# A two-layer recurrent mixture-of-experts kernel: final combination, load order and output scatters moved by a block, and a reshaped last pass

## The reference, cut to what matters

```
gate_scores = softmax(xn @ Wg + bg);  topk = top 2 of 8 experts, weights normalised
for e in range(8):
    h = gelu(xn @ W1[e] + b1[e])          # 256 -> 1024
    y = h @ W2[e] + b2[e]                 # 1024 -> 256
    output = output + y * combine_w[..., e:e+1]
g = silu(output)
x = x + s * g                             # s: the layer's attention part; x is the result
```

## Time and profile before

| | us |
|---|---|
| median of 3 runs | 1163.1 |
| lowest and highest of them | 1156.14, 1164.56 |
| the profiled execution, its own time | 1147.92 |
| its span | 1145.8 |
| PE busy in the span | 1033.5 (90%) |

### The profile page before, as it was taken

How to read it: one execution, slowest core, us unless ns; L and a number is a source line. 1 busy time by engine, 2 the same in 40 slices (tenths; PEclk the granted TensorE clock), 3 DMA queues, 4 the chain that set the end, 5 groups by cost and what they waited for, 6 DMA issues and landing times.

```text
span 1145.8 us, 16791 instructions
## 1 busy us (share of the span) xinstructions
PE 1033.5 (90%) x6152; PEld 887.7 (77%) x6152; DVE 692.3 (60%) x1494; ACT 528.7 (46%) x1095; POOL 404.3 (35%) x385
## 2 busy tenths in 40 slices
PE   4559899999999984879899999999999999999993
PEld 3347788888888863568788898988888888888882
DVE  7578777777777858587754644474766100137862
ACT  4425654555545536643344545445453233345641
POOL 1036544554455450001233422322231345432344
PEclk9779999999999997997899999999999999999997
DMA  9914335555565428426487755555244679889961
GB/s 302 265 61 148 93 102 175 162 162 176 162 201 184 122 90 270 160 92 232 111 286 280 249 192 187 191 189 189 106 132 182 218 266 342 322 319 337 395 266 65
DMA packets 120401, 228.65 MB, mean 200 GB/s; under 512 B 14938, under 2 KB 103914, under 8 KB 115328
## 3 DMA queue, kind: packets, MB, share of 16 engines
q1 hardware_dynamic: 106448, 189.31, 48.2%
q0 software_dynamic: 13872, 38.27, 10.3%
HBM read 166.98 MB, written 62.79 MB: 201 GB/s over the span
## 4 chain that ended last, share of the span: by engine, by line
PE 74%; DVE 14%; ACT 5%; DMA 3%; issue 2%; POOL 1%; SPq 1%; POOLq 0%; ACTq 0%; DVEq 0%
PE PS L1306 21%; PE PS L1316 20%; PE PS L1205 6%; PE PS L1090 4%; PE PS L1040 3%; PE PS L1144 3%; PE PS L1099 2%; PE PS L1171 2%; PE PS L1215 2%; PE PS L1182 2%; PE PS L1157 2%; DVE stats L1347 2%; PE PS L1281 1%; PE PS L1292 1%; DVE KB L1482 1%
## 5 line engine op out<-in xcount | busy, mean ns | idle before, releaser
L1306 PE MATMUL PS<-xgT,WE 128*128 128x256 f32 (+1 forms) x1248 | 257.5, 364 | 4.3 <-ACT hT L2255 3.6
L2255 ACT ACTIVATE hT<-PS,WE 128x256 f32<-128x256 f32 (+1 forms) x312 | 140.2, 454 | 237.9 <-PE PS L1306 234.8
L1306 PEld LDWEIGHTS PS<-xgT,WE 128*128 128x128 f32 x1248 | 221.4, 192 | 33.5 <-ACT hT L2255 5.7
L1316 PE MATMUL PS<-WE,hT 128*128 128x256 f32 x1104 | 244.6, 379 | 0.0
L1316 PEld LDWEIGHTS PS<-WE,hT 128*128 128x128 f32 x1104 | 207.6, 190 | 26.8
L1909 DVE TENSOR_TENSOR y<-PS,WE 128x512 f32<-128x512 f32 (+1 forms) x38 | 24.3, 640 | 221.2 <-PE PS L1316 221.2
L2355 POOL DMA_INDIRECT xg<-xn_dram,token_of x71 | 74.2, 1045 | 142.2 <-DVE result_of L1825 116.2
L2367 POOL DMA_INDIRECT result<-y,result_of x53 | 53.7, 1013 | 178.6 <-DVE y L1909 171.5
L1040 PE MATMUL PS<-XT,Wf 128*128 128x256 f32 x384 | 93.6, 399 | 3.3 <-ACT Z L2033 3.3
L1040 PEld LDWEIGHTS PS<-XT,Wf 128*128 128x128 f32 x384 | 74.9, 201 | 15.1 <-ACT Z L2033 4.9
L2314 POOL TENSOR_TENSOR prob<-prob,row_sum 128x512 f32<-128x512 f32 x56 | 58.6, 1046 | 60.2 <-DVE row_sum L1520 59.9
(11 more groups left out here) (276 smaller groups left out, 1720.5 us busy)
## 6 DMA issues: line engine op xcount, KB each, us to landing
WE<-in_experts SPq DMA_DIRECT2D x39, 2180.0 KB, 9.4
wgu<-in_w_gate SPq DMA_DIRECT2D x32, 256.0 KB, 2.9
wgu<-in_w_up SPq DMA_DIRECT2D x32, 256.0 KB, 3.2
wdn<-in_w_down SPq DMA_DIRECT2D x32, 256.0 KB, 3.4
result<-zeros SPq DMA_DIRECT2D x16, 512.0 KB, 4.8
xs<-late_dram SPq DMA_DIRECT2D x16, 512.0 KB, 12.9
both<-result SPq DMA_DIRECT2D x16, 512.0 KB, 9.7
table<-zeros POOLq DMA_DIRECT2D x1, 5160.0 KB, 34.1
```

The lines of the kernel that those rows point to most:

```text
L1306: m = e.matmul(PS[:, FIRST_H_BANK + nth % HR, 0:rows], W1[n % WR][:, k, c * P:(c + 1) * P], xgT[:, n % 2, k, 0:rows], start=k == 0, stop=k ...
L1316: m = e.matmul(PS[:, u.bank, j * D:(j + 1) * D], hT[:, n % 2, c, j * P:(j + 1) * P], W2[n % WR][:, c, :], start=c == 0, stop=c == KF - 1)
L2255: e.activation(hT[:, n % 2, c, 0:rows], PS[:, FIRST_H_BANK + (KF * n + c) % HR, 0:rows], ACT.Gelu_apprx_tanh, bias=b1[n % WR][:, c:c + 1], ...
```

## The change

What it does, by part:

1. `load_both(0..2)` is placed ahead of `load_weights(32)` in block 29's list.
2. `MIXED_AT` loses its empty first entry: the quarters are worked in blocks 30 to 35 (one, two, one, two, one, one), each one late block earlier, though not with the same grouping.
3. `load_xs(5..7)` leave the `store` step; they now follow `load_weights` of the block after the one in which the place's quarter was stored: quarter 5's in block 31, quarters 6's and 7's in block 32.
4. The scatters of late blocks 30 to 33 go to block 35's list, those of 34 and 35 to block 36's, that of 36 to block 37's, that of 37 to block 38's, each behind that block's gather `late_other`; that of 38 stays last. As `LAGGED` is 35 now, `late_sum`, `late_gate` and `late_rest` of blocks 34 to 36 change place too: 35's whole pass stands in block 36, ahead of its own `w2` bank's emptying.
5. Last block: the bias is no longer added when the bank is emptied. `late_bias` adds own weight times `b2` to the scaled other row before the matmuls end; `late_end` then has one sum out of PSUM, a half product that needs no gate, and two more instructions behind the gate.

```
-MIXED_AT = [[], [0, 1], [2], [3], [4, 5], [6], [7]]
+MIXED_AT = [[0], [1, 2], [3], [4, 5], [6], [7]]
 LAGGED = EARLY + len(MIXED_AT) - 1
-PUT_FIRST, PUT_SECOND = 4, 6
+PUTS_AT = {LAGGED: range(0, 4), LAGGED + 1: range(4, 6), LAGGED + 2: range(6, 7), LAST: range(7, 8)}
...
-        if n == LAST - 1:
-            for m in range(PUT_FIRST, PUT_SECOND):
-                add("late_put", EARLY + m)
         if EARLY <= n + 1 < NSLOT:
             add("late_other", n + 1)
-        if n == LAST - 2:
-            for m in range(PUT_FIRST):
-                add("late_put", EARLY + m)
-        if n == LAST - 1:
-            for m in range(EARLY + PUT_SECOND, LAST):
-                add("late_put", m)
+        for m in PUTS_AT.get(n, ()):
+            add("late_put", EARLY + m)
+        if n + 1 == EARLY:
+            for q in range(BR):
+                add("load_both", q)
         if n + WR < NSLOT:
...
                 add("load_weights", n + WR)
+        for q in MIXED_AT[n - 1 - EARLY] if EARLY < n <= LAGGED else ():
+            if q + XSR < QUARTERS:
+                add("load_xs", q + XSR)
         if XS_AT <= n < XS_AT + XSR:
             add("load_xs", n - XS_AT)
-        if n + 1 == EARLY:
-            for q in range(BR):
-                add("load_both", q)
...
+        def late_bias():
+            i = LAST - EARLY
+            w.wait_ge(weights_in[LAST % WR], weights1_landed(LAST))
+            w.wait_ge(late_step, late_n.n)
+            for j in range(2):
+                tile = 2 * i + j
+                e.scalar_tensor_tensor(out=other[i % OR][:, j, :], in0=b2[LAST % WR], scalar=own_weight[:, tile:tile + 1],
+                                       in1=other[i % OR][:, j, :], op0=ALU.mult, op1=ALU.add).then_inc(
+                    late_step, late_n.step())
+            wait_place_free(w, LAST)
+
+        def late_end(j):
+            i, u = LAST - EARLY, use["w2_last", j]
+            tile = 2 * i + j
+            z, half, gate = other[i % OR][:, j, :], y1[:, LAST % YR, j, :], gate_late[:, j, :]
+            filled_by(u)
+            w.wait_ge(late_step, late_n.n)
+            e.scalar_tensor_tensor(out=z, in0=PS[:, u.bank, 0:D], scalar=own_weight[:, tile:tile + 1], in1=z, op0=ALU.mult,
+                                   op1=ALU.add).then_inc(late_summed, 1)
+            w.wait_ge(late_summed, tile + 1)
+            e.scalar_tensor_tensor(out=half, in0=z, scalar=0.5, in1=fin[:, tile, D:2 * D], op0=ALU.mult, op1=ALU.mult).then_inc(
+                late_step, late_n.step())
+            w.wait_ge(late_step, late_n.n)
+            w.wait_ge(late_gated, tile + 1)
+            e.scalar_tensor_tensor(out=half, in0=gate, scalar=1.0, in1=half, op0=ALU.add, op1=ALU.mult).then_inc(
+                late_step, late_n.step())
+            w.wait_ge(late_step, late_n.n)
+            e.tensor_tensor(fin[:, tile, 0:D], fin[:, tile, 0:D], half, ALU.add).then_inc(late_ready, 1)
...
                 j, = at
-                u = use["w2_last", j]
                 if j == 0:
                     late_scale(LAST)
-                filled_by(u)
-                w.wait_ge(weights_in[LAST % WR], weights1_landed(LAST))
-                wait_place_free(w, LAST)
-                e.tensor_tensor(y1[:, LAST % YR, j, :], PS[:, u.bank, 0:D], b2[LAST % WR], ALU.add).then_inc(free[u.bank], 1)
-                w.wait_ge(free[u.bank], u.emptied)
-                late_sum(LAST, j)
-                late_rest(LAST, slice(j, j + 1))
+                    late_bias()
+                late_end(j)
...
                 if q + BR < QUARTERS:
                     load_both(q + BR)
-                if q and q - 1 + XSR < QUARTERS:
-                    load_xs(q - 1 + XSR)
```

More of the change, by code:

```diff
@@ L1614, in late_sum @@
             tile = 2 * i + j
-            u = use["w2_last", j] if n == LAST else use["w2", n]
+            u = use["w2", n]
             w.wait_ge(free[u.bank], u.emptied)
```

## The result

The changed kernel takes 1150.16 us (median of 12 runs, 1145.28 to 1155.94), the kernel before 1158.86 us on the same chip (12 runs, 1156.14 to 1164.56): ratio 0.9919, 95% interval 0.9900 to 0.9939. It is 8.7 us faster. Forecast were 1157 us, a range from 1151 to 1165, and a gain of 5.8 us.

The account below looks back on a forecast made before the run. PE was taken to bound the kernel up to a serial tail of 8.91 us; 6.0 - 0.4 + 0.2 = 5.8 us gained, ratio 0.995, scaled from the median 1163.1 to 1157 us, range 1151 to 1165.

Parts of the forecast that it names:

- Scatters spread (part 4): Tail: block 38's gather is issued by 1119.5 us, so VectorE's 5.44 us of idleness before block 38 go entirely.
- Last pass (part 5): Last block: last scatter at 1129.9 against 1135.98 us, a gain of 6.1, taken as 6.0; removed instructions 0.9.
- Sums ahead of weights (part 1): Block 29: second scatter lands in 2.7 us, so the loads of sums leave at 1004.5 instead of 1009.60 us.
- Quarter 0 in block 30 (part 2): Blocks 30 and 31: `both(0)` lands at 1010.5 us, limit 1012.1, no wait; with slow scatters PE waits 3.5 us.
- DMA load (part 3): Block 36's weights: half a megabyte more ahead of them, 0.4 us more wait, bounds 0 to 2.5.
- Block 35's pass in block 36: ScalarE's gate ahead of block 37's GELUs: ready at 1097.7 us, limit 1101; no wait unless the gather is 3 us later.
- The sum: Whole kernel: 6.0 - 0.4 + 0.2 = 5.8 us gained, profiled execution from 1147.92 to 1142.1 us, ratio 0.995.
- No case gains more than 6.5 us, because PE's end stays.: All cases: 6.5 us is the largest gain, since PE's end fixes the rest of the tail.
- the scaling: Whole time: profiled execution is 1.3% below the median 1163.1 us, so 1163.1 x 0.995 = 1157.

Follow-up runs that it names:

- chip 7: Kernel before and changed kernel run again, both unchanged: ratio 0.9944, 1140.3 against 1147.5 us; block 30's `w1` start to last scatter 130.75 against 136.91 us.
- the first trace: Profile of the unaltered changed kernel from the first measurement: execution 1153.15 us, block 30's `w1` start to last scatter 135.02 us against 137.15 before.
- The slow variant: Changed kernel with the three loads of sums behind block 32's weights, as before: ratio 0.9993 to the kernel before.
- With more load: Both kernels with five extra 512 KB writes, one ahead of each of weights 33 to 37: ratios 1.0013 (kernel before) and 0.9999 (changed).
- chip 8: Slower chip, both kernels run unchanged: changed kernel at ratios 0.9922, 0.9932 and 0.9915, the last 1147.8 against 1157.8 us.

## Why the prediction was right and wrong

- **Scatters spread (part 4): right.** Gather of block 38 at +118.2 on chip 7 (forecast: near +118), no idle time of VectorE between blocks 37 and 38. Undone alone: 2.68 us of the gain.
- **Last pass (part 5): right.** 2.75 us from PE's end to the last scatter (forecast 2.8), 6.16 us gained where 6.0 were taken.
- **Sums ahead of weights (part 1): right**, and shown by undoing it: the scatters land in 2.4 us (forecast 2.7) instead of 7.6, the sums leave at +5.5 (forecast +5.7). Weights 32 land 3.5 us before they are wanted on chip 7 (forecast 4.3).
- **Quarter 0 in block 30 (part 2): right in effect, its margin mis-sized.** `both(0)` landed at +12.4 in the first trace and on chip 7; forecast was +11.7, limit +13.3, since the load took 6.9 us from the first issue and not 6.0. The slow variant cost 3.52 us, the forecast 3.5.
- **DMA load (part 3): mis-sized.** 0.4 us of wait were taken, none came; weights 36 had 0.4 us to spare. (The sum takes 0.4 us of wait "more" and yet gives back today's 0.23, which don't go together; without the 0.2 it is 5.6.) With more load the wait does come in block 36, 4.9 us of it.
- **Block 35's pass in block 36: right**, no wait.
- **The sum, in the stretch: right where TensorE's results come in time.** 6.2 us against 5.8, ratio 0.9944 on chip 7.
- **The statement that failed: "No case gains more than 6.5 us, because PE's end stays."** On the slower chip what hangs on PE's end doesn't stay: its last results are late in the last 25 us, in both kernels, by 4.0 us of the stretch in the kernel before and 2.1 in the changed one on chip 8. With this the measured 8.7 us are 6.2 + 0.3 + some 2. That the first comparison's chip is like chip 8 is argued from its times and from the changed kernel's trace, which lost 4.3 us in this way; no trace shows the kernel before in that comparison. So the 2 us are measured on chip 8 and argued for the first comparison.
- **The step that put the time out of the range: the scaling.** "Its own time is 1.3% below the median, 1163.1, so I scale" took the median of three runs. Twelve runs have 1158.86, so 4.2 of the 6.8 us by which the forecast was too high come from there, and 2.9 from the larger gain, less 0.3 of rounding. By 1158.86 x 0.995 it would have been 1153.1, and the range 1147 to 1161. The traced execution was 15 us faster than the median and 8 us faster than the fastest timed run, and just what the kernel takes on the three faster chips: a sign that it hadn't what the timed ones had. It was read as a factor.

## What to carry to other kernels

Take the tail and the front of a change separately: here all 6 us are in the tail, and the reordering in front of it only makes that tail possible without a new wait, but its first part undone alone costs 3.8 us of the stretch. Before issuing a large load beside a small scatter that something waits for, see whether the load can leave behind the wait. When the traced execution is over 1% faster than the timed runs, it may come from another chip, and some stretch in the timed runs may be longer in a way that the trace doesn't show; the bounds of a forecast have to leave room for a change of that stretch too.

## What was not expected of the hardware

- Chips differ by 1% on the same kernel (medians of 1147.0 to 1147.5 us on three, 1157.1 to 1158.9 on chip 8 and in the first comparison), and 3.5 to 4.5 us of it are TensorE's results arriving late in the last 25 us, the last one by 8.9 us in one trace. Another 2.3 and 4.8 us lie ahead of block 30 (1002.88 and 1005.31 on chip 8 against 1000.56 on chip 7) and weren't looked into.
- Matmul rows of 7.07 us, on time, can stand in such a trace; the spacing of the GELUs behind them (0.86 or 1.4 us) shows the lateness. Whether the matmuls or only their signals were late takes a second look: three GELUs within 1.20 us, 0.14 us behind the block before, can't be parts that were just computed at 0.86 us each.
- A rest of PE can cost more than itself. After 3.52 us the clock still read 1.00 and nothing more was lost; after 4.32 and 4.88 us it read 0.69 and 0.65, and the next `w1` piece took 6.27 us instead of 4.58, the next whole `w1` 8.52 instead of 7.07.
